# A fused attention and mixture-of-experts kernel: the loads, constants and weight copies at its beginning are rearranged

## The reference

```python
def rms_norm_multihead(x, weight):
    normed = x * rsqrt(mean(x * x, axis=-1, keepdims=True) + 1e-8)
    return normed * weight

# attention, on X = layernorm(x)
K = X.reshape(B, L, H, d)
Q = rms_norm_multihead((X @ Wq.T).reshape(B, L, H, d), q_norm_w)
V = rms_norm_multihead((X @ Wv.T).reshape(B, L, H, d), v_norm_w)
W = cumsum(einsum('blhd,blhe->blhde', K, V), axis=1)
x = x + einsum('blhd,blhde->blhe', Q, W).reshape(B, L, D)

# feed-forward, on xf = layernorm(x)
weights, indices = top_k(softmax(xf @ Wg), 4)
y = for each expert: its rows, swiglu(rows, W1[e], W2[e], W3[e]) * weight, added back
x = x + y + swiglu(xf, Ws1, Ws2, Ws3)
```

## Time and profile before

| what | value |
|---|---|
| three runs | 563.85, 562.59, 558.1 us; median 562.59 us |
| profiled execution | 559.33 us |
| its span, first to last instruction | 557.4 us |
| mean granted TensorE clock | 0.983 of full |
| PE, DVE, ACT, POOL busy | 527.4, 382.2, 376.5, 331.8 us |

### The profile page before, as it was taken

One profiled execution on the slowest core, in us unless ns is written; L12 is line 12 of the kernel. 1 busy time (PEld: TensorE's weight loads), 2 busy tenths in 40 slices (PEclk: granted clock), 3 DMA queues, 4 the chain that ended last, 5 costly groups with the idle time before them and its releaser, 6 DMA issues.

```text
span 557.4 us, 18176 instructions
## 1 busy us (share of the span) xinstructions
PE 527.4 (95%) x5177; PEld 383.1 (69%) x5177; DVE 382.2 (69%) x1354; ACT 376.5 (68%) x1258; POOL 331.8 (60%) x367
## 2 busy tenths in 40 slices
PE   6798999999999999699999999999999999997996
PEld 2355666666666665357998988999999995544554
DVE  7698999999999996664444444444444446744786
ACT  2687899988989985402766766777677776653452
POOL 6010377776777777771665555666666564446992
PEclk8999999999999999899999999999999999998999
DMA  8998355556456554954676776766666554428999
GB/s 259 316 292 264 125 217 211 187 215 227 186 198 246 188 192 152 366 194 127 195 219 201 221 225 199 214 193 194 194 193 198 180 187 145 143 79 342 408 409 347
DMA packets 65088, 123.29 MB, mean 221 GB/s; under 512 B 9824, under 2 KB 44000, under 8 KB 64992
## 3 DMA queue, kind: packets, MB, share of 16 engines
q1 hardware_dynamic: 47824, 78.07, 44.1%
q0 software_dynamic: 13056, 39.86, 19.2%
q10 hardware_dynamic: 4112, 4.19, 2.3%
HBM read 58.49 MB, written 63.60 MB: 219 GB/s over the span
## 4 chain that ended last, share of the span: by engine, by line
PE 79%; DMA 5%; DVE 4%; issue 4%; ACT 3%; POOL 2%; SPq 1%; ACTq 1%; DVEq 0%; POOLq 0%
PE pS L967 18%; PE pQV L828 10%; PE pS L985 9%; PE pS L741 8%; PE pS L795 5%; PE pO L888 5%; DMA xg<-xs 3%; PE pO L869 3%; PE pT L946 3%; PE pQV L946 2%; PE pQV L757 2%; PE pO L757 2%; PE pT L774 2%; PE pO L803 2%; PE pT L817 1%
## 5 line engine op out<-in xcount | busy, mean ns | idle before, releaser
L495 POOL DMA_INDIRECT ys<-gsh,dst x144 | 138.1, 959 | 108.3 <-ACT gsh L663 86.6
L467 POOL DMA_INDIRECT xs<-xg,posi x128 | 123.8, 967 | 52.1 <-issue 31.4
L967 PE MATMUL pS<-after_a,x2T_all 128*128 128x128 f32 x1024 | 135.5, 276 | 0.0
L967 PEld LDWEIGHTS pS<-after_a,x2T_all 128*128 128x128 f32 x1024 | 124.5, 192 | 0.0
L1375 DVE TENSOR_TENSOR after_a<-after_a,pS 128x128 f32<-128x128 f32 x144 | 41.5, 288 | 79.9 <-ACT after_a L651 76.1
L1346 DVE COPY x2T_all<-w 128x512 f32 x144 | 63.9, 444 | 32.9 <-issue 32.5
L985 PE MATMUL pS<-w,after_a 128*128 x256 | 76.7, 381 | 0.0
L1089 DVE TENSOR_TENSOR w<-pS,tri 128x512 f32<-128x512 f32 x96 | 65.1, 679 | 1.0 <-PE pS L795 1.0
L828 PE MATMUL pQV<-w 128*128 128x512 f32 x128 | 63.7, 621 | 0.5 <-ACT w L533 0.5
L663 ACT ACTIVATE gsh<-pS,xg 128x256 f32<-128x256 f32 x128 | 60.6, 474 | 0.4 <-issue 0.4
L662 ACT CAST dst<-xg 128x1 int32 x128 | 24.5, 191 | 45.3 <-PE pS L985 43.3
(11 more groups left out here) (221 smaller groups left out, 1019.8 us busy)
## 6 DMA issues: line engine op xcount, KB each, us to landing
xg<-xs SPq DMA_DIRECT2D x128, 160.0 KB, 2.8
ys<-gsh SPq DMA_DIRECT2D x32, 512.0 KB
w<-ys SPq DMA_DIRECT2D x32, 512.0 KB, 15.3
w<-in_L_ffn_W ACTq DMA_DIRECT2D x1, 4096.0 KB, 18.6
out<-xall SPq DMA_DIRECT2D x14, 256.0 KB, 7.2
xs<-padrow SPq DMA_DIRECT2D x32, 80.0 KB
xg<-xs SPq DMA_DIRECT2D x32, 80.0 KB, 2.2
ys<-gsh,dst POOLq DMA_INDIRECT x144
```

What stands on the lines that cost most here:

```text
L467: pool.indirect_dma_start(out=xs, out_offset=bass.IndirectOffsetOnAxis(ap=posi[:, a.r8, k:k + 1], axis=0), in_=xr[:, a.r8, :], in_offset=N ...
L495: pool.indirect_dma_start(out=ys, out_offset=bass.IndirectOffsetOnAxis(ap=dst[:, j % 8:j % 8 + 1], axis=0), in_=y[:, j % 8, :], in_offset= ...
L967: last = pe.matmul(pS[a.b][:, n * P:(n + 1) * P], w13_staged(a.t)[:, (2 * k + n) * F:(2 * k + n + 1) * F], xgT[:, a.b, k, :], start=(k == ...
```

## The change

Five things change at the beginning:

1. SP loads x tile 0 alone (new semaphore `x_head`), then tiles 1 to 3 (`x_first`).
2. Wq and Wv are issued by ACT, ahead of its table load, instead of by SP.
3. DVE clears `w_bd` first, and PE's `keep_busy` waits for that alone. DVE then takes the statistics of tile 0 ahead of the constants, makes only three constants (`par_i`, `par_f` twice) and the bias of tile 0, and makes the other eleven constants behind the statistics of tiles 1 to 3.
4. POOL's `rstd1(0)` stands ahead of the four masks of `head_mask`.
5. ACT copies only the first half of the transposed weights; DVE copies the second.

```diff
--- before.py
+++ after.py
@@ -300,7 +300,7 @@
             return early.get((g, m, n), pS[2 * m + n])
 
 
-        names = """x_first x_second x_third x_rest w_in wc_in wg_in ident_done consts_pool consts_dve zeros_dve wt_ps wt_done
+        names = """x_head x_first x_second x_third x_rest w_in wc_in wg_in ident_done consts_pool consts_dve zeros_dve wt_ps wt_done
             stats1 mean1 var1_done rstd1 nb1_done xn_done xnT_ps xnT_done qv_ps sq_done ss_done ln_done guess_done newta newtb rms_done
             qn_done v_done qT_ps qm_done qT_done state_ps state_done scores_ps masked o1_ps o_ps oT_done
             ot_ps x2_done stats2 mean2 var2_done nb2_done xr_done x2T_ps x2T_done lgT_ps lgT_done logits_ps
@@ -331,9 +331,8 @@
 
         @block.sync
         def _(sp):
-            sp.dma_start(xall[:, 0:4, :], x_tiles[:, 0:4, :]).then_inc(S["x_first"], 16)
-            sp.dma_start(wq_in, Wq.rearrange("(k p) c -> p k c", p=P)).then_inc(S["w_in"], 16)
-            sp.dma_start(wv_in, Wv.rearrange("(k p) c -> p k c", p=P)).then_inc(S["w_in"], 16)
+            sp.dma_start(xall[:, 0:1, :], x_tiles[:, 0:1, :]).then_inc(S["x_head"], 16)
+            sp.dma_start(xall[:, 1:4, :], x_tiles[:, 1:4, :]).then_inc(S["x_first"], 16)
             sp.dma_start(xall[:, 4:8, :], x_tiles[:, 4:8, :]).then_inc(S["x_second"], 16)
             for wc, w in ((wqc, q_norm_w), (wvc, v_norm_w)):
                 for g in range(KC):
@@ -443,6 +442,7 @@
             chain(pool.affine_select(out=tri[:], in_=tri[:], compare_op=ALU.is_ge, fill=0.0, base=0,
                                      pattern=[[1, P]], channel_multiplier=-1))
             chain(pool.memset(head_mask[:], 1.0))
+            rstd1(0)
 
             for base, mult in ((0, 1), (d - 1, -1)):
                 for g in range(KC):
@@ -450,7 +450,6 @@
                     chain(pool.affine_select(out=v, in_=v, compare_op=ALU.is_ge, fill=0.0, base=base,
                                              pattern=[[-d * mult, HG], [0, d]], channel_multiplier=mult))
             assert c[0] == HEAD_CONSTS
-            rstd1(0)
             rstd1(1)
             chain(pool.memset(padrow[:], 0.0))
             rstd1(2)
@@ -504,6 +503,8 @@
         @block.scalar
         def _(act):
 
+            act.dma_start(wq_in, Wq.rearrange("(k p) c -> p k c", p=P)).then_inc(S["w_in"], 16)
+            act.dma_start(wv_in, Wv.rearrange("(k p) c -> p k c", p=P)).then_inc(S["w_in"], 16)
             act.preload_act_table_set("natural_log_exp_and_others")
 
             def normalise(t):
@@ -517,9 +518,8 @@
                 act.activation(xn[:, t % 3, :], xall[:, t, :], ACT.Identity, bias=bias, scale=scale).then_inc(S["xn_done"], 1)
 
             normalise(0)
-            for k in range(KC):
-                act.wait_ge(S["wt_ps"], k + 1)
-                act.copy(wqv[:, k, :], (pT0, pT1)[k][:]).then_inc(S["wt_done"], 1)
+            act.wait_ge(S["wt_ps"], 1)
+            act.copy(wqv[:, 0, :], pT0[:]).then_inc(S["wt_done"], 1)
 
             def copy_scores(a, j):
                 wait(act, S["scores_ps"], 4 * a.t + j + 1)
@@ -1028,17 +1028,30 @@
                 dve.scalar_tensor_tensor(out=nb1[:, t:t + n], in0=mv1[:, t:t + n, 0], scalar=-1.0,
                                          in1=rs1[:, t:t + n], op0=ALU.mult, op1=ALU.mult).then_inc(S["nb1_done"], 1)
 
+            dve.memset(w_bd[:], 0.0).then_inc(S["zeros_dve"], 1)
             dve.memset(vp, 0.0)
-            dve.memset(w_bd[:], 0.0)
             dve.memset(v8[:], 3.0e38)
             dve.memset(ss[:], 1.0)
             dve.memset(cst[:], 2.0 * E * STR)
             dve.memset(lens[:], 0.0)
             dve.memset(eps_col[:], RMS_EPS).then_inc(S["zeros_dve"], 1)
+            dve.wait_ge(S["x_head"], 16)
+            stats1(0)
+            mean1(0)
             dve.wait_ge(S["consts_pool"], 6)
             chain(dve.tensor_scalar(par_i[:], par_i[:], 4, 1, ALU.logical_shift_right, ALU.bitwise_and))
             chain(dve.tensor_copy(par_f[:, 1:2], par_i[:]))
             chain(dve.tensor_scalar(par_f[:, 0:1], par_f[:, 1:2], -1.0, 1.0, ALU.mult, ALU.add))
+            bias1(0)
+            dve.wait_ge(S["wt_ps"], 2)
+            dve.tensor_copy(wqv[:, 1, :], pT1[:]).then_inc(S["wt_done"], 1)
+            dve.wait_ge(S["x_first"], 16)
+            stats1(1)
+            mean1(1)
+            stats1(2)
+            mean1(2)
+            stats1(3)
+            mean1(3)
             chain(dve.tensor_copy(eidx[:], eidx_i[:]))
             chain(dve.tensor_scalar(ebase[:], eidx[:], float(STR), None, ALU.mult))
             chain(dve.tensor_scalar(ecap[:], eidx[:], float(STR), float(CAP), ALU.mult, ALU.add))
@@ -1050,16 +1063,6 @@
             chain(dve.tensor_scalar(jm[:], jm[:], -float(E), None, ALU.add))
             chain(dve.tensor_scalar(place[:, 0:1], jc[:, 0:1], 2.0, None, ALU.mult))
             chain(dve.tensor_scalar(place[:, 1:2], jc[:, 1:2], float(2 * NU - E // 2), None, ALU.add))
-            dve.wait_ge(S["x_first"], 16)
-            stats1(0)
-            mean1(0)
-            stats1(1)
-            mean1(1)
-            stats1(2)
-            mean1(2)
-            bias1(0)
-            stats1(3)
-            mean1(3)
             dve.wait_ge(S["x_second"], 16)
             stats1(4)
             mean1(4)
@@ -1067,7 +1070,7 @@
             for t in range(5, lead_a):
                 stats1(t)
                 mean1(t)
-            dve.wait_ge(S["zeros_dve"], 1)
+            dve.wait_ge(S["zeros_dve"], 2)
             dve.wait_ge(S["consts_pool"], HEAD_CONSTS + 1)
             dve.wait_ge(S["wc_in"], 64)
             dve.wait_ge(S["ident_done"], 2)
```

## The result

The changed kernel takes 566.4 us (median of 4 runs, 565.46 to 567.69), the kernel before 561.09 us (median of 4, 558.1 to 563.85). The interval doesn't hold 1: the change made the kernel slower, by 5 to 6 us. The profiled execution of the changed kernel took 567.15 us.

What follows compares the result with a forecast made beforehand. PE, busy 527.4 of 557.4 us, was taken to bound the kernel. A first sum of squares 2.4 us later plus 1.3 us of lower clock, 3.7 us, on the mean of 561.0 gave 564.7 us; range 559.7 to 569.5.

Steps and rivals of the forecast that it cites:

- The sign and the mechanism: First stage: kernel slower, as DVE's late constants and added weight copy delay tile 0's sum of squares despite earlier PE work.
- The loads: Start: x tile 0 lands at 4.0 us (bounds 3.7 to 4.7), Wv at about 6.2 as before (bounds 4.7 to 6.9).
- The term of DVE: DVE, tile 0: sum of squares starts at 16.7 in place of 14.28, 2.4 us later; bounds +0.9 to +3.1.
- from 6.2 to 7.3: PE's weight transposes at the start: claimed to run in this interval, taking 1.09 us.
- 3.60 us of work without a gap: DVE, from the bias of tiles 1 to 3 to the first sum of squares: unchanged work, putting the sum at 16.7.
- The transposes of xn: PE, tile 0: start at 8.05 in place of 9.35, 1.3 us earlier, with DVE's weight copy taken as 0.6 us.
- The clock: PE, tile 1's product: after 3 us idle, more than 1.9, it runs at the lower clock, 3.28 us, costing 1.3 us.
- Rival 2: PE, tile 1's product: the clock holds through the longer idle time; 563.4 us, chance 0.22.
- rival 3: PE's products: the clock falls and stays down, 1.3 us per tile; 567.3 us at three tiles, chance 0.08.
- rival 1: First stage: the 1.3 us gain from the weight copies comes out at the end; 559.7 us, chance 0.12.
- Rival 4: Behind the first stage: the loss is given back because something further on keeps its own time; 561.0 us, chance 0.10.
- The sum: Whole kernel: 2.4 us from DVE plus 1.3 us from the clock, 3.7 us later; 564.7 us forecast, chance 0.48.

Runs made afterwards that it cites:

- filling the gap: Changed kernel with six occupying products in place of two between tile 1's xn transposes and tile 0's q transposes; ratio to the kernel before 1.003, then 1.0066 when repeated.
- constants back, alone: Kernel before, with only the eleven DVE constants moved from ahead of tile 0's statistics to behind tile 3's; 559.94 us against 559.26, ratio 1.0018.
- constants into idle time: Changed kernel with its eleven late DVE constants placed between tile 0's bias and the wait for the transposed weights; 562.69 us against 559.26, ratio 1.0051.
- clearing earlier: Changed kernel with GpSimd's clearing of 1024 columns moved ahead of its root for tiles 1 to 3; 565.15 us, ratio to the kernel before 1.0118.
- third occupying product: Changed kernel with three occupying products at PE's start in place of two; 566.27 us, ratio to the kernel before 1.0114.
- split copy alone: Kernel before, with only the second half of the transposed weights copied by DVE, behind tile 0's bias; 708.93 us against 707.74, ratio 1.0015.
- weights from SyncE: Changed kernel with Wq and Wv issued by SyncE again, between x tiles 1 to 3 and 4 to 7; ratio to the kernel before 1.0077.

## Why the prediction was right, point by point

**The sign and the mechanism** were right: the weight copy and the normalise of tile 0 left the chain, and DVE's list, with the constants moved into it, took their place. Moving the constants back into the idle time gave 2.3 us, 1.5 of them up to the bias of tiles 1 to 3 and 0.8 behind it, for another reason. The loads did as forecast for Wv (6.2), and no gain of the second queue can be seen (6.30 with it, 6.41 without, scatter 0.2). From 3.8 to 5.6 us the two queues together moved 372 GB/s, one queue alone 373 in the kernel before. x tile 0 was at 3.5, 0.5 us earlier than taken and also ahead of the lower bound of 3.7; this brought nothing, as DVE then waited for PE longer.

**The term of DVE** was mis-sized: 2.4 us forecast, 3.9 measured, over the upper bound of 3.1. Two things were missing. The weight transposes took 0.9 us more, because PE hadn't come up to speed by 6.3 in that execution; the prediction carried over the 1.09 us of the trace before and gave no price to a slow PE there. By the other profiles this is as much chance as change: three of seven executions have it. And 0.7 us came from the table row's copy meeting GpSimd's clearing. The steps that were mis-sized are thus PE's "from 6.2 to 7.3" for the weight transposes and the "3.60 us of work without a gap" from the bias of tiles 1 to 3 to the sum of squares, which took 4.4 us: a list of durations moved in time doesn't keep its durations when another engine's work moves against it. Before, the copy ended 0.1 us into the clearing (11.88 to 12.06 against 11.99). In the changed kernel it began 0.2 us into it. The reason isn't the masks that the change moved on GpSimd, which the prediction rightly called free: the constants alone, with GpSimd's list as before, gave the same 0.89 us. By the rows, it is that the bias no longer waits for GpSimd's root (0.59 us before) and that GpSimd now waits for the statistics of tile 4, so the two lists lie differently to each other: behind the bias of tiles 1 to 3 the copy began after 2.3 us in place of 2.2, the clearing after 2.2 in place of 2.3.

**The transposes of xn** came 0.3 us earlier and not 1.3, for the same 0.9 us and since the copy took 0.69 us, not 0.6 (its rows gave 0.44 and 0.68). It didn't matter, as said.

**The clock** was right in place and size: 3.94 us idle (3 forecast), 3.53 us for the product (3.28 forecast), 1.6 us of loss (1.3 forecast). Its rule, that an idle time longer than the 1.9 us of before costs the clock and a shorter one doesn't, is not shown: filling the gap avoided the loss in one execution and not in the other. That the forecast came true here is in part luck. Rival 2 (the clock holds) is out for the changed kernel's profile, rival 3 (it stays down) too, as only one tile was slow; rival 1 (the gain goes through) is out by DVE's timeline. Rival 4 (given back) is out as a whole: the last product into pQV starts 5.8 us later (201.7 to 207.5 us). On the way, though, the distance to the kernel before shrank to 4.7 us by tile 7 and grew again (see Open), so the prediction's "from there on the same distances" holds only roughly.

**The sum**: 3.7 us forecast, 5.4 at the marker (3.9 and 1.6), 5.3 between the medians; 564.7 us forecast, 566.4 measured. It came to lie at the threshold of 1% that I had given 0.11.

**Open:** the marker isn't what arrives at the end. How much later than in the kernel before the products into pQV start, in the profiles of the first round, and the expert stage from the first to the last of its first products (L967), in us:

| kernel | tile 3 (marker) | tile 7 | last product into pQV | expert stage | span |
|---|---|---|---|---|---|
| before | | | | 199.9 | 557.4 |
| constants back, alone | +3.0 | +0.8 | +1.5 | 199.5 | 557.8 |
| constants into idle time | +3.1 | +1.6 | +2.6 | 200.5 | 559.6 |
| clearing earlier | +3.5 | +2.8 | +4.1 | 201.3 | 563.2 |
| changed | +5.4 | +4.7 | +5.8 | 202.1 | 565.2 |
| third occupying product | +5.7 | +3.5 | +4.6 | 202.4 | 565.7 |

Up to 2.2 us are given back between tiles 3 and 7. 0.7 us of that is common to all versions. The rest, up to 1.5 us, goes with a pause of PE for which the profile shows no wait. The kernel before (first line) and the changed kernel (second) both have it, behind the product of tile 5:

```profile
43.26 0.31 PE L869 MATMUL pO<-w,w_bd 128*32 128x128 f32 x3 [1.08 <-issue]
```

```profile
48.69 0.31 PE L869 MATMUL pO<-w,w_bd 128*32 128x128 f32 x3 [1.08 <-issue]
```

The version with the clearing moved has the same 1.08 us, the one with the constants in the idle time 0.25, the other two none. I have no cause for it. The span grew by 7.8 us, 2 more than at the end of the attention stage, and these lie in the expert stage. It is longer the later the kernel is, from 199.5 to 202.4 us, nearly in order; six profiles can't tell whether the late beginning lengthens it or chance does, and no run tests it. Why the time with the clearing moved is no better than the changed kernel's, with a marker 1.9 us better, stays open with it.

## What to carry to other kernels

Before moving work out of the front of an engine's list, look at what the engine will do in the time set free. Here it stood idle for over 4 us waiting for x, a root and PE, while 2.3 us of constants that fitted exactly there had been put behind the wait; order by when inputs arrive, not by importance. And an engine that is made earlier without the one that it waits for becomes idle for longer, and the product behind the longer idle time can be slow: in two of the partial versions (constants back alone, split copy alone) the product of tile 1 took 1.7 and 1.0 us more.

## What the runs showed of the hardware

- A DVE copy of 128x32 from int32 to float32 within SBUF takes 0.18 us, and 0.89 us when it starts while GpSimd is clearing 128x1024: it ends when GpSimd ends, while GpSimd loses 0.07 us (1.02 in place of 0.95). A copy of 128x2 took 0.33 us in place of 0.19 in the same way, in the changed kernel, when GpSimd cleared 128x320 (12.23 to 12.59). Statistics of 128x256 that lay wholly within the clearing, in the kernel before (12.17, in 11.99 to 12.94), took 0.42 us as ever. In the thirteen profiles the copy of 128x32 took 0.89 us the six times that it started within the clearing, and 0.18 the other seven. By what way the clearing holds a copy up, and why not the statistics, no run here shows.
- Float32 products of 128x512 (4 matmuls) took 1.96 us at a granted clock of 1.00 (product of tile 1 before) and 3.78 at 0.50 (product of tile 0, weights from SyncE); 3.53 us went with 0.55 on average. Behind 3.0 to 3.9 us of idle time that of tile 1 took 2.96 to 3.69 us, in five profiles. But the length of the idle time doesn't decide alone: 2.0 us lost the clock ahead of the product of tile 0 in the kernel before (3.28 us), and 2.45 us kept it for tile 1 with the constants in the idle time. With the gap filled, the clock fell in one of two executions with no idle time over 1.2 us since.
- At the start of an execution PE ran at half speed at first (two occupying products took 3.78 us in the changed kernel, 1.88 from 14.89 on), while the profile's column shows a granted clock of 1.00. In the same beginning it came up to speed at different times: the weight transposes, 0.95 to 1.5 us behind the end of the occupying products, took 1.97 us in three executions and 1.09 in four.
